# Quantised attention on one Trainium2 core: where a unit's second half of values is multiplied

## The chip, the core and the metric

The kernel runs on one core of a Trainium2 chip. The core has five engines that run side by side, each with its own queue in order: TensorE (PE, matrix products into PSUM; its weight loads are listed apart as PEld), VectorE (DVE), ScalarE (ACT), GpSimd (POOL) and SyncE (SP), which here issues the DMA transfers. They wait for each other by semaphores. The metric is the device time of one execution in microseconds, lower is better.

## What is computed

Two layers of a perceiver: a float cross attention with 16 heads of 128, a channel-mixing layer, an expert layer, then in the second layer a cross attention whose operands are quantised, a dilated self attention and a feed-forward in a block format. The part that the change touches is the quantised cross attention:

```python
q = _fq_sym(q, axis=-1)          # 16 heads of 16
k = _fq_sym(k, axis=-1)
v = _fq_sym(v, axis=2)
attn = jnp.einsum('bhqd,bhkd->bhqk', q, k)
attn = jax.nn.softmax(attn.astype(jnp.float32), axis=-1)
attn = _fq_unsigned(attn, axis=-1)       # 0..255 steps of the row's largest
out = jnp.einsum('bhqk,bhkd->bhqd', attn, v)
```

There are 2 batches of 128 queries, 16 heads, and 4096 keys (the contexts of both batches together).

## The kernel before, in words

A unit is one batch and one head: 32 units, of 128 queries against 4096 keys. Their stage runs from about 456 us to 658 us of the span; before it lies the float cross attention, behind it a tail. Work on a unit has these steps:

- **First scores** (`pe_first`, L1845): TensorE computes the scores in 8 blocks of 512 keys, each into one of three PSUM banks; VectorE reduces each block to the rows' largest value (`dve_first`, L1889, reduction at L1891). These run ahead: in quarter q of unit u TensorE computes blocks 8u+12+2q and the next, that is blocks of units u+1 and u+2. A bank is written again when the reduction three blocks earlier has ended (`q_max`).
- GpSimd folds the eight values into the exponential's bias (L2009 to L2016).
- **Second scores** (`pe_second`, L1861): TensorE computes the same scores again, 1024 keys (a quarter) at a time, into one of two pairs of banks; ScalarE makes the exponential of the quarter (L1884) into a row buffer of halves (`y`, in the space named cT in the profile), two quarters to a half. The quarter two later may be computed when this exponential has ended (`q_exp`).
- **Transposition**: when both quarters of a half are there, SyncE issues a DMA transpose of 128 x 2048 values (L1979) into `yT` (in the space named c_nat). Its landing is told by one of four semaphores, q_turned00 to q_turned11: parity of the unit, then half.
- **Values** (`attend`, product at L1907): 16 matmuls of 128 x 16 for each half, which add up in PSUM bank 7. This is done two units behind: in unit u for unit u-2. All score matmuls are recorded at L1842, first and second alike.

TensorE's order is written out in `pe_attention` (L1895): unit by unit, four quarters each, in each quarter two second-score matmuls, two first-score matmuls, then what else belongs there. Between these steps lies a second program, `side`, whose pieces have slots in quarters 1 to 3 of each unit and work on other layers: mixing, experts and queries of batch 1, then the output, the dilated attention and the feed-forward of batch 0. In quarter 0 TensorE only waits there for the engine that empties the last piece's room in bank 7. ScalarE, VectorE and GpSimd weave their parts of `side` in the same way. SyncE's own queue also loads weights for later in units 0 to 4 (`sp_ahead`, L1449 to L1454).

Units are counted below as the loop does (u from 1); the values multiplied in unit u are those of unit u-2.

Of the kernel before, what the change touches and what calls it, by code (L numbers as in the profile page):

```python
# [43 lines left out]
UNITS = B * H0  # L44
# [20 lines left out]
NH = KT * P // HALF  # L65
# [415 lines left out]
def pe_idle_product(pe, m, ps):  # L481
    return pe.matmul(ps, m.ident_fp16[:, :], m.kT[:, 0, 0:BLK], start=True, stop=True)
# [1362 lines left out]
def pe_first(pe, m, s, n):  # L1845

    if n == 0:
        pe.wait_ge(s["exp"], UNITS)
    if n % NB == 0 and n // NB % H1 < KG:
        pe.wait_ge(s[f"qu_act{n // (NB * H1)}"], QU_ACT[f"qT{n // NB % H1}"])  # L1850
    if n > 2:
        pe.wait_ge(s["q_max"], n - 2)
    pe_scores(pe, m, n // NB, m.bank(n % 3), n % NB * BLK).then_inc(s["q_first"], 1)
# [7 lines left out]
def pe_second(pe, m, s, u, q):  # L1861

    n = NC * u + q
    if u == 0 and q > 0:
        pe.wait_ge(s["q_exp"], q)
    elif n == NC:
        pe.wait_ge(s["q_exp"], NC)
    elif n > NC:
        pe.wait_ge(s["q_exp"], n - 1)
    if n == NC + 1:  # L1870
        pe.wait_ge(s["added"], UNITS)
    for k in range(CHUNK // BLK):
        ins = pe_scores(pe, m, u, m.bank(second_place(u, q) + k), q * CHUNK + k * BLK)
    ins.then_inc(s["q_second"], 1)
# [20 lines left out]
def pe_attention(pe, m, x, s, side):  # L1895
    def attend(z, half):
        b, h = z // H1, z % H1
        if z < UNITS - 1:
            pe.wait_ge(s[f"q_turned{z % 2}{half}"], 16 * (z // 2 + 1))
        else:  # L1900
            pe.wait_ge(s["q_back_dve"], NB // 2 if half == 0 else BACK_DVE)
        if z == UNITS - 1 and half == 1:
            pe.wait_ge(s["q_back_act"], NB - BACK_DVE)
        if z in (H1, H1 + H1 // 2) and half == 0:
            pe.wait_ge(s["at_dve0"], AT_DVE["over_sum1" if z > H1 else "over_sum0"])
        for j in range(KT // NH):
            ins = pe.matmul(m.bank(7)[:, h * HD1:(h + 1) * HD1], x.yT[:, z % 2, half * KT // NH + j, :],  # L1907
                            m.v_int[:, half * KT // NH + j, h * HD1:(h + 1) * HD1], start=half == 0 and j == 0,
                            stop=half == 1 and j == KT // NH - 1)
        ins.then_inc(s["q_pv"], 1)  # L1910

    def turn(n):

        pe.wait_ge(s["q_exp"], NC * (UNITS - 1) + n * BLK // CHUNK + 1)
        if n == 3:
            pe.wait_ge(s["q_back_dve"], 1)
        if n == 0:
            pe.wait_ge(s["q_max"], NB * UNITS)
        y = m.y[:, (UNITS - 1) % 2, n * BLK:(n + 1) * BLK]
        for j in range(BLK // P):  # L1920
            ins = pe.matmul(m.bank(back_bank(n))[:, j * P:(j + 1) * P], y[:, j * P:(j + 1) * P], m.ident_fp16[:, :],
                            start=True, stop=True)
        ins.then_inc(s["q_back"], 1)
        if n == NB - 1:
            pe.wait_ge(s["q_back_dve"], 3)
            for _ in range(2):
                pe_idle_product(pe, m, m.bank(2))

    pe.wait_ge(s["v_rounded_dve"], KT // 4)
    pe.wait_ge(s["v_rounded_pool"], KT // 4)  # L1930
    for u in range(1, UNITS + 2):
        for q in range(NC):
            if u < UNITS:
                pe_second(pe, m, s, u, q)
            for n in range(AHEAD + NB * u + 2 * q, AHEAD + NB * u + 2 * q + 2):
                if n < NB * UNITS:
                    pe_first(pe, m, s, n)
            if q == 0:
                side.upto(NC * u - 0.5)
            if u >= UNITS and q < 2:  # L1940
                for n in range(NB // 4 * (2 * (u - UNITS) + q), NB // 4 * (2 * (u - UNITS) + q + 1)):
                    turn(n)
            if u > 1 and q < 2:
                attend(u - 2, q)
            if q > 0:
                side.upto(NC * u + q)

# [13 lines left out]
def back_bank(n):  # L1961

    return n % 3 if n < NB // 2 else n - 1
# [551 lines left out]
def perceiver(nc, t):  # L2515
    pe, act, dve, pool, sp = nc.tensor, nc.scalar, nc.vector, nc.gpsimd, nc.sync
    with ExitStack() as stack:
# [28 lines left out]
        with ExitStack() as local:  # L2546
# [13 lines left out]
                pool_output(pool, m, y, a, s, 0, 1, room, output), pool_dilated(pool, m, s, 0, room, dilated),  # L2560
                pool_feed(pool, m, w, s, 0, room, feed), pool_output(pool, m, y, a, s, 1, 0, room, output_last)))
            pe_attention(pe, m, y, s, Side(
                pe_mix(pe, m, x, s, 1, room, mix), pe_experts(pe, m, s, 1, room, experts, a.expert_wT),
                pe_queries(pe, m, s, 1, room, queries), pe_output(pe, m, y, a, s, 0, 0, room, output),
# [71 lines left out]
```

## Time and profile before

| | |
|---|---|
| median of 3 runs | 691.06 us (691.05 to 693.09) |
| profiled execution | 691.99 us, of which the traced span is 690.6 us |
| busy in the span | PE 94%, DVE 83%, ACT 60%, POOL 57% |
| chain of waits over the span | PE 64%, DVE 17%, ACT 5%, DMA 5%, POOL 4% |
| attention stage, 560 to 652 us (92 us) | PE busy 83.7, DVE 87.5, ACT 83.3, POOL 42.8 |

Busy time of PE counts overlapping matmuls as one stretch and their ends are modelled, so a busy PE is not necessarily a full one. The chain of waits is followed back from the last instruction: each step is what released it. A row of the chain "PE psum L1842 x4" is four score matmuls in a row.

### The profile page before, as it was taken

How to read it: one execution, taken by the hardware profiler on the slowest of the kernel's cores; microseconds unless marked ns; L12 is line 12 of the kernel's file. 1: busy time of each engine (PE TensorE's matmuls, PEld its weight loads, DVE VectorE, ACT ScalarE, POOL GpSimd, SP SyncE). 2: the span in 40 equal slices, each digit the busy share in tenths (PEclk: the TensorE clock that was granted, in tenths of full speed). 3: DMA queues.
4: the chain of work that ended last, by engine and by line, in shares of the span. 5: the costliest groups of instructions: out<-in, count | busy, mean ns of one | idle time of the engine just before them, and what ended most of it. 6: DMA issues, size and time to landing. Idle time of an engine off the chain costs nothing.

```text
span 690.6 us, 13892 instructions
## 1 busy us (share of the span) xinstructions
PE 651.4 (94%) x5088; PEld 410.2 (59%) x5088; DVE 575.2 (83%) x1029; ACT 417.4 (60%) x695; POOL 391.5 (57%) x504
## 2 busy tenths in 40 slices
PE   9899999999999999989999999989889989988887
PEld 7456666667666676756776667754346434544453
DVE  5998987897798797889989769888877889999655
ACT  5654454444544465655574445448878889899941
POOL 5877666577557627689956515527634543345401
PEclk9999999999999999999999999999999999999999
DMA  9666789756647689988885984739998989999900
GB/s 314 155 149 127 164 176 180 164 137 144 138 117 154 144 177 224 208 186 178 163 182 124 184 173 110 157 81 211 222 207 153 165 139 203 167 182 164 196 19 9
DMA packets 347971, 111.27 MB, mean 161 GB/s; under 512 B 313592, under 2 KB 344576, under 8 KB 347904
## 3 DMA queue, kind: packets, MB, share of 16 engines
q1 hardware_dynamic: 347904, 110.39, 77.6%
q8 instruction: 41, 0.67, 0.4%
q14 instruction: 26, 0.21, 0.1%
HBM read 32.23 MB, written 0.26 MB: 47 GB/s over the span
## 4 chain that ended last, share of the span: by engine, by line
PE 64%; DVE 17%; ACT 5%; DMA 5%; POOL 4%; issue 3%; SPq 2%; POOLq 0%; ACTq 0%; DVEq 0%
PE psum L1059 19%; PE psum L1031 18%; DVE tops L1891 7%; PE psum L1842 6%; PE psum L1045 5%; PE psum L506 3%; ACT cT L1884 3%; PE psum L1907 2%; DMA wqk_h<-in_wkT 2%; DMA c_nat<-cT 2%; DVE neg_max L1271 1%; DMA c_nat<-in_expert_wT 1%; PE psum L1084 1%; PE psum L1094 1%; PE psum L826 1%
## 5 line engine op out<-in xcount | busy, mean ns | idle before, releaser
L1059 PE MATMUL psum<-c_nat,eT 128*128 128x256 f16 x1536 | 188.1, 273 | 0.9 <-ACT u_sb L1233 0.9
L1891 DVE TENSOR_REDUCE tops<-psum 128x1 f32<-128x512 f32 x256 | 159.6, 683 | 20.2 <-PE psum L1842 19.5
L1884 ACT ACTIVATE cT<-psum,bias,q_scale 128x1024 f16<-128x1024 f32 x128 | 153.7, 1205 | 22.0 <-PE psum L1842 20.3
L1031 PE MATMUL psum<-cT,qk 128*128 128x512 f16 x744 | 165.6, 379 | 0.1
L1059 PEld LDWEIGHTS psum<-c_nat,eT 128*128 128x128 f16 x1536 | 147.3, 98 | 24.1 <-issue 1.6
L1842 PE MATMUL psum<-kT,v_space 128*128 128x512 f16 x512 | 139.5, 387 | 9.2 <-DVE tops L1891 7.3
L1031 PEld LDWEIGHTS psum<-cT,qk 128*128 128x128 f16 x744 | 72.6, 98 | 82.3 <-issue 1.2
L1271 DVE TENSOR_REDUCE neg_max<-psum 128x1 f32<-128x2048 f32 x32 | 73.2, 2287 | 21.9 <-PE psum L1031 21.8
L1259 DVE TENSOR_TENSOR e_lo<-e_all,e_hi 128x2048 f16<-128x2048 f32 x32 | 88.8, 2774 | 0.0
L1842 PEld LDWEIGHTS psum<-kT,v_space 128*128 128x128 f16 x512 | 45.2, 98 | 70.8 <-DVE tops L1891 34.2
L1202 ACT ACTIVATE e_all<-psum,neg_max 128x2048 f32<-128x2048 f32 x32 | 63.1, 1971 | 16.0 <-DVE neg_max L1273 16.0
L857 ACT ACTIVATE qT<-psum 128x128 f32<-128x128 f32 x31 | 8.7, 279 | 103.8 <-PE psum L826 94.2
L775 POOL TENSOR_TENSOR k_full<-k_int,k_scale 128x256 f32<-128x256 bf16 x32 | 21.7, 679 | 70.7 <-DVE k_int L1339 47.0
L1207 ACT CAST e_hi<-e_all 128x2048 f16<-128x2048 f32 x32 | 60.8, 1900 | 1.5 <-DMA eT<-e_hi 0.6
L2011 POOL TENSOR_SCALAR least<-least,tops 128x1 f32<-128x1 f32 x64 | 23.3, 364 | 50.3 <-DVE tops L1891 49.3
L1045 PE MATMUL psum<-wkv,cT 128*128 128x512 f16 x192 | 46.7, 379 | 2.5 <-DVE k_tmp L1325 2.5
L776 POOL TENSOR_TENSOR k_parts<-k_int,k_scale 128x256 f16<-128x256 bf16 x32 | 48.8, 1524 | 0.0
L1907 PEld LDWEIGHTS psum<-v_space,c_nat 128*128 128x128 f16 x1024 | 33.8, 96 | 22.8 <-DMA c_nat<-cT 6.6
L745 POOL TENSOR_TENSOR u_parts<-u_sb,u_parts 128x256 f16<-128x256 f32 x30 | 31.4, 1046 | 24.3 <-ACT u_parts L1238 24.3
L1907 PE MATMUL psum<-v_space,c_nat 128*128 128x16 f16 x1024 | 35.3, 170 | 8.7 <-DMA c_nat<-cT 4.4
L748 POOL TENSOR_TENSOR wvo_parts<-wvo_h,wvo_parts 128x512 f16<-128x512 f32 x30 | 36.6, 1219 | 0.1
L758 POOL TENSOR_TENSOR wqk_parts<-wqk_h,wqk_parts 128x512 f16<-128x512 f32 (+1 forms) x27 | 31.0, 1147 | 2.5 <-ACT wqk_parts L869 2.1
(287 smaller groups left out, 946.9 us busy)
## 6 DMA issues: line engine op xcount, KB each, us to landing
wvo_h<-in_L_xattn_Wv SPq DMA_DIRECT2D x30, 128.0 KB, 2.4
wvo_h<-in_L_xattn_Wo SPq DMA_DIRECT2D x30, 128.0 KB, 2.4
wqk_h<-in_L_xattn_Wq SPq DMA_DIRECT2D x28, 128.0 KB, 2.5
wqk_h<-in_wkT SPq DMA_DIRECT2D x28, 128.0 KB, 2.8
mx_land<-in_mx_weights SPq DMA_DIRECT2D x8, 384.0 KB, 3.8
v_space<-in_ctx SPq DMA_DIRECT2D x4, 512.0 KB, 5.5
cT<-in_ctx SPq DMA_DIRECT2D x2, 1024.0 KB, 8.0
c_nat<-in_expert_wT SPq DMA_DIRECT2D x2, 1024.0 KB, 7.8
```

The source lines that it names most:

```text
L776: pool.tensor_tensor(hi, ints, scale, ALU.mult).then_inc(s["k_cut"], 1)
L1031: ins = pe.matmul(s_ps[:, n * 512:(n + 1) * 512], c.qk[:, u % 2, q_part, k, :], m.cT[:, b, c_part, 4 * n:4 * n + 4, k, :], start=(k, q_par ...
L1045: ins = pe.matmul(kv_ps, m.cT[:, kt // KTB, c_part, kt % KTB, k, :], d.wkv[w_part][:, k, :], start=(k, w_part, c_part) == (0, 0, 0), stop= ...
L1059: ins = pe.matmul(u_ps, c.eT[:, v % 2, e_part, j, :], m.c_nat[:, v // H0, c_part, j, :], start=(j, e_part, c_part) == (0, 0, 0), stop=(j, ...
L1202: act.activation(c.e_all[:, :], s_ps, ACT.Exp, bias=c.neg_max[:, u % 2:u % 2 + 1], scale=1.0 / UP, accum_out=c.row_sum[:, u:u + 1]).then_i ...
L1207: act.copy(c.e_hi[:, :], c.e_all[:, :]).then_inc(s["e_hi"], 1)
L1259: dve.tensor_tensor(c.e_lo[:, :], c.e_all[:, :], c.e_hi[:, :], ALU.subtract).then_inc(s["e_lo"], 1)
L1271: dve.tensor_reduce(limit, s_ps, AX.X, ALU.max, negate=True).then_inc(s["max"], 1)
L1842: return pe.matmul(ps, m.qT[:, b, group, r, :], m.kT[:, group, at:at + BLK], start=True, stop=True)
L1884: act.activation(m.y[:, u % 2, q * CHUNK:(q + 1) * CHUNK], m.bank(second_place(u, q), 2), ACT.Exp, bias=m.bias[:, u:u + 1], scale=m.q_scal ...
L1891: dve.tensor_reduce(m.tops[:, n // NB, n % NB:n % NB + 1], m.bank(n % 3), AX.X, ALU.max, negate=True).then_inc(s["q_max"], 1)
L1907: ins = pe.matmul(m.bank(7)[:, h * HD1:(h + 1) * HD1], x.yT[:, z % 2, half * KT // NH + j, :], m.v_int[:, half * KT // NH + j, h * HD1:(h ...
```

## The change

In `pe_attention` the call that multiplies the second half of unit u-2's values is issued in quarter 0 of unit u, right behind the first half, and no longer in quarter 1. For the two last turns (u = 32 and 33, where no new scores are computed) the halves stay in quarters 0 and 1. Nothing else changes: the instructions, buffers, banks and the other engines' programs are the same.

```diff
-            if u > 1 and q < 2:
-                attend(u - 2, q)
+            for half in range(NH) if 1 < u < UNITS and q == 0 else (q,) if u >= UNITS and q < NH else ():
+                attend(u - 2, half)
             if q > 0:
                 side.upto(NC * u + q)
```

NH is 2, UNITS is 32. So it moves 16 matmuls in each of the 30 units 2 to 31, on TensorE alone.

In TensorE's queue, unit 7 (values of unit 5) before; q_turned10 and q_turned11 are the landings of the two halves:

```order
L1842 MATMUL psum<-kT,v_space 128x512 [waits q_exp]
L1842 MATMUL psum<-kT,v_space 128x512
L1842 MATMUL psum<-kT,v_space 128x512 [waits q_max] x2
L1907 MATMUL psum<-v_space,c_nat 128x16 [waits q_turned10,mix_act1]
L1907 MATMUL psum<-v_space,c_nat 128x16 x15
L1842 MATMUL psum<-kT,v_space 128x512 [waits q_exp]
L1842 MATMUL psum<-kT,v_space 128x512
L1842 MATMUL psum<-kT,v_space 128x512 [waits q_max] x2
L1907 MATMUL psum<-v_space,c_nat 128x16 [waits q_turned11]
L1907 MATMUL psum<-v_space,c_nat 128x16 x15
```

and with the change:

```order
L1842 MATMUL psum<-kT,v_space 128x512 [waits q_exp]
L1842 MATMUL psum<-kT,v_space 128x512
L1842 MATMUL psum<-kT,v_space 128x512 [waits q_max] x2
L1907 MATMUL psum<-v_space,c_nat 128x16 [waits q_turned10,mix_act1]
L1907 MATMUL psum<-v_space,c_nat 128x16 x15
L1907 MATMUL psum<-v_space,c_nat 128x16 [waits q_turned11]
L1907 MATMUL psum<-v_space,c_nat 128x16 x15
L1842 MATMUL psum<-kT,v_space 128x512 [waits q_exp]
L1842 MATMUL psum<-kT,v_space 128x512
L1842 MATMUL psum<-kT,v_space 128x512 [waits q_max] x2
```

The wait for q_turned11 and its 16 matmuls moved ahead of two second-score and two first-score matmuls.

In TensorE's queue, unit 16 (values of unit 14), from a piece of the side program (L2080) on, before:

```order
L2080 MATMUL psum<-wp,xnT 128x256 [waits wp1_scaled,at_act0]
L1842 MATMUL psum<-kT,v_space 128x512 [waits q_exp]
L1842 MATMUL psum<-kT,v_space 128x512
L1842 MATMUL psum<-kT,v_space 128x512 [waits q_max] x2
L1907 MATMUL psum<-v_space,c_nat 128x16 [waits q_turned00,at_act0]
L1907 MATMUL psum<-v_space,c_nat 128x16 x15
L1842 MATMUL psum<-kT,v_space 128x512 [waits q_exp]
L1842 MATMUL psum<-kT,v_space 128x512
L1842 MATMUL psum<-kT,v_space 128x512 [waits q_max] x2
L1907 MATMUL psum<-v_space,c_nat 128x16 [waits q_turned01]
L1907 MATMUL psum<-v_space,c_nat 128x16 x15
L1842 MATMUL psum<-kT,v_space 128x512 [waits q_exp]
```

and with the change:

```order
L2080 MATMUL psum<-wp,xnT 128x256 [waits wp1_scaled,at_act0]
L1842 MATMUL psum<-kT,v_space 128x512 [waits q_exp]
L1842 MATMUL psum<-kT,v_space 128x512
L1842 MATMUL psum<-kT,v_space 128x512 [waits q_max] x2
L1907 MATMUL psum<-v_space,c_nat 128x16 [waits q_turned00,at_act0]
L1907 MATMUL psum<-v_space,c_nat 128x16 x15
L1907 MATMUL psum<-v_space,c_nat 128x16 [waits q_turned01]
L1907 MATMUL psum<-v_space,c_nat 128x16 x15
L1842 MATMUL psum<-kT,v_space 128x512 [waits q_exp]
L1842 MATMUL psum<-kT,v_space 128x512
L1842 MATMUL psum<-kT,v_space 128x512 [waits q_max] x2
L1842 MATMUL psum<-kT,v_space 128x512 [waits q_exp]
```

Here the same four score matmuls moved behind 16 more matmuls of L1907; from the quarter after them on, the queue is as it was.

## Rows read from the trace of the kernel before

**Rows 1.** Stretches of the attention stage: start:end, length, busy time by engine

```profile
core 0: us, PE busy (x) PEld busy (x) DVE busy (x) ACT busy (x) POOL busy (x), PEclk, DMA share, GB/s
...
560.00:652.00 92.00, 83.70 (x818) 41.83 (x817) 87.49 (x169) 83.31 (x147) 42.76 (x105) 0.99 1.04 179
```

**Rows 2.** Costliest groups, 470 to 652 us: | busy us, mean ns | idle

```profile
L1891 DVE TENSOR_REDUCE tops<-psum 128x1 f32<-128x512 f32 x232 | 144.3, 683 | 16.6 <-PE psum L1842 16.1
L1884 ACT ACTIVATE cT<-psum,bias,q_scale 128x1024 f16<-128x1024 f32 x118 | 141.7, 1204 | 16.1 <-PE psum L1842 14.4 <-issue 0.5 <-DMA c_nat<-cT 0.3
L1842 PE MATMUL psum<-kT,v_space 128*128 128x512 f16 x464 | 126.1, 388 | 8.2 <-DVE tops L1891 7.3 <-ACT v_space L1811 0.2 <-ACT cT L1884 0.2
...
L1907 PE MATMUL psum<-v_space,c_nat 128*128 128x16 f16 x933 | 32.2, 170 | 7.6 <-DMA c_nat<-cT 4.4 <-ACT v_space L1811 1.6 <-DVE mid L2303 1.1
```

**Rows 3.** Timeline in unit 16: start, us, engine, line, names, count

```profile
564.55 4.55 DVE L1891 TENSOR_REDUCE tops<-psum 128x1 f32<-128x512 f32 x7
...
565.29 0.56 PE L1907 MATMUL psum<-v_space,c_nat 128*128 128x16 f16 x16
...
565.71 1.02 PE L1842 MATMUL psum<-kT,v_space 128*128 128x512 f16 x4
...
566.57 0.55 PE L1907 MATMUL psum<-v_space,c_nat 128*128 128x16 f16 x16
...
566.97 2.37 PE L1842 MATMUL psum<-kT,v_space 128*128 128x512 f16 x9
```

**Rows 4.** Chain of waits, 510 to 652 us, by line

```profile
by line: DVE tops L1891 32.3%; PE psum L1842 22.7%; ACT cT L1884 8.0%; PE psum L1907 7.0%; PE psum L506 4.0%; issue 3.8%; ACT v_space L1811 1.2%; DVE mx_amax L2233 1.1%; POOL xn L464 0.9%; PE psum L2180 0.9%; DVE mid L2303 0.8%; DVE stats L
```

**Rows 5.** Chain of waits in order: start, us, what

```profile
525.46 0.88 PE psum L1842 x4
526.34 0.38 PE psum L1907 x16
...
565.85 0.68 PE psum L1842 x3
...
566.55 5.54 DVE tops L1891 x9
...
572.82 5.98 DVE tops L1891 x10
```

**Rows 6.** Chain of waits, units 14, 21 and 24

```profile
553.50 0.25 PE psum L1792 x4
...
595.54 0.68 PE psum L1842 x3
...
596.25 0.69 DVE tops L1891
...
613.11 0.46 PE psum L1842 x2
...
613.59 0.97 ACT cT L1884
```

**Rows 7.** Timeline of TensorE, unit 19: a block that waits for its bank

```profile
582.63 0.39 PE L1842 MATMUL psum<-kT,v_space 128*128 128x512 f16 x1 [0.21 <-DVE tops L1891]
```

**Rows 8.** Who waited for whom, 470 to 652 us: total, times, longest

```profile
PE psum L1907 <- DMA c_nat<-cT: 4.4, 4, 2.4
```

**Rows 9.** SyncE's timeline, 483 to 508 us

```profile
497.78 11.32 SPq L1979 DMA_TRANSPOSE c_nat<-cT  x4
```

**Rows 10.** Unit 7: timeline of TensorE

```profile
503.61 1.02 PE L1842 MATMUL psum<-kT,v_space 128*128 128x512 f16 x4
...
507.00 0.56 PE L1907 MATMUL psum<-v_space,c_nat 128*128 128x16 f16 x16 [2.37 <-DMA c_nat<-cT]
```

**Rows 11.** Transpositions (L1979), 510 to 652 us, us to landing

```profile
DMA to landing us min/median/max: 4.2/4.5/6.6
```

**Rows 12.** The one transposition issued at 575.6 us

```profile
DMA to landing us min/median/max: 6.6/6.6/6.6
```

**Rows 13.** Windows: the stretch behind that wait, columns as in rows 1

```profile
507.40:511.70 4.30, 4.30 (x20) 1.63 (x17) 3.00 (x7) 2.87 (x5) 1.79 (x3) 0.60 1.15 232
```

## The prediction

> **What bounds the kernel now.** I read first the busy time by stretch. From 560 to 652 us, 92 us and some 15 units, VectorE is busy 87.5 us, TensorE 83.7 and ScalarE 83.3 [rows 1]: three engines within 5% of each other, none with room for a delay of its own. The groups give the pieces [rows 2]: a reduction of a block takes 683 ns, an exponential 1,204 ns, a score matmul 388 ns and a value matmul 170 ns, but matmuls overlap, so their price must be read from starts.
>
> The timeline of unit 16 does that [rows 3]. The 16 value matmuls of a half start at 565.29 and the next score matmul at 565.71; at 566.57 and 566.97 again. So a half holds TensorE for **0.41 us**. Four score matmuls (a quarter's second and first scores) hold it from 565.71 to 566.57, **0.86 us**. VectorE's row there is 7 reductions in 4.55 us, 0.65 each, near 0.63 where more stand in a row: 1.25 us for the two blocks of a quarter. Thus quarters 0 and 1 take TensorE 0.86 + 0.41 = 1.27 us each, quarters 2 and 3 take 0.86 plus side work. That is just VectorE's 1.25 and ScalarE's 1.2 us. The layout before spreads the halves evenly.
>
> The chain of waits from 510 to 652 us has 32.3% on the reductions, 22.7% on score matmuls, 8.0% on exponentials and 7.0% on value matmuls [rows 4]: it changes engines all the time, and what a delay costs depends on where the chain is between the two halves.
>
> **What the change does.** No instruction is added or removed. In each of 30 units, 16 matmuls, 0.41 us, move ahead of four score matmuls. They are TensorE's only; no DMA is issued otherwise, and SyncE, VectorE, ScalarE and GpSimd keep their order. In quarter 0 TensorE then works 1.68 us and in quarter 1 0.86; behind the old place it is where it was. So quarter 1's second scores (the input of ScalarE's exponential) and first scores (two reductions) come 0.41 us later, and nothing comes earlier except bank 7's sums, for which nobody waits in these units. That has four kinds of outcome.
>
> *The chain stays on TensorE across both places: no cost.* An example is unit 10, with value matmuls, four score matmuls, value matmuls in a row on the chain [rows 5]; the 0.41 us is only reordered. Units 3, 10 to 12, 15, 20 and 27 look like this. I charge 0 for them, and 0 also where VectorE has side work queued (units 13 and 22, whose reductions start over 0.6 us after their scores are there). The cover is the wait of VectorE in quarter 2 that the trace shows in units 10 and 11; without it each would pay up to 0.41.
>
> *The chain leaves TensorE right after the first half, to an engine that waits for it: full price.* In unit 16 the chain goes value matmuls, three score matmuls (565.85), then VectorE at 566.55 for nine reductions in a row, then after a short piece of side work ten more from 572.82 [rows 5]. The third score matmul is the first block of quarter 1. It comes 0.41 us later, and VectorE has nothing else. Unit 21 (595.54 to 596.25) is the same, and in unit 24 two score matmuls release the exponential of quarter 1 at 613.59, from which side work hangs [rows 6]. I find six such units: 16, 21, 24, 25, 26 and 30. 6 x 0.41 = 2.5 us.
>
> *The chain is on VectorE, with TensorE held back by the banks.* A score block may be written when the reduction three blocks back has ended; at that moment VectorE has two blocks ready and gets this one, 3 x 0.63 = 1.9 us of work. Until quarter 1's first block is there TensorE needs 0.21 (this matmul) + 0.41 (first half) + 0.43 (second scores) + 0.38 (the block itself) = 1.43 us, and about 0.2 goes for the signal, as in the row of a block that waits for its bank, 0.21 [rows 7]. That leaves 0.2 to 0.3 us of slack, and 0.41 is asked: 0.2 us lost in each of units 9, 17, 23 and 29, 0.8 us. Where TensorE was a little late already (units 8, 18 and 28) 0.2 to 0.3 each, 0.7 us together. It isn't won back in quarter 2, since there VectorE never waits in these units.
>
> *The second half has not landed.* Four waits of TensorE for a transposition stand in the stage, 4.4 us, the longest 2.4 [rows 8]. They are in units 5 to 7, where SyncE's queue is behind: it issues four transpositions in a row in 11.3 us from 497.78 on [rows 9], long after their exponentials. So these landings don't move with TensorE. In unit 7 TensorE computes quarter 1's four score matmuls at 503.61, then waits for the half until 507.00 [rows 10]. With the change it waits first and has these four left at 507.4: **0.86 us later** for all that follows, since the chain runs over this landing and then on TensorE. In units 5 and 6 the same happens, but SyncE's backlog of over 3 us hides it: 0.
>
> Elsewhere the margin is this. The half's transposition is issued when its last exponential ends and lands 4.5 us later in the median, 6.6 at most [rows 11]. At the new place TensorE stands three quarters of a unit of 6 us plus 1.3 us after that exponential, 5.8 us. Only landings above this are late; the one issued at 575.6 (6.6 us, [rows 12]) is, by some 1.1 us, in unit 19, and a wait of 0.3 us may come in unit 17. In unit 19 VectorE has side work; I charge 0.2 us. On the other side, in unit 14 the chain enters TensorE between the two halves and reaches a product of the side program (553.50, [rows 6]) behind the second: that comes up to 0.41 us earlier; I take 0.2. These two cancel.
>
> **Sum.** 2.5 + 0.8 + 0.7 + 0.9 = +4.9 us. Against the profiled execution, 691.99 us with a span of 690.6, that is 696.9 with a span of 695.5. The profiled one lies 0.9 above the median of 691.06, so for the median I say **696.0 us**. Bounds: only the zero-slack units and unit 7, less 0.8 us for TensorE's shorter way to side work in units 14 and 19, give +2.6; 0.41 in each of 20 units without cover gives 8.2, so 699.3.
>
> A rule speaks against this. The stretch from 560 to 652 us shows weight loads busy 41.8 of 92 us [rows 1]. The Trainium skill (Perfetto Trace Analysis, Identifying the Most-Contended Engine) has TensorE's headroom judged by weight-load busy share and not by matmul busy time. By it TensorE is at 45% and could take 0.41 us anywhere: the sum would be the first rival's. By the rows of starts TensorE is full in quarters 0 and 1, and I go by these.
>
> **Rivals.**
> (1) *The delay is absorbed, no change.* The exponential and the reduction double- and triple-buffer, and VectorE idles 4.5 of the 92 us; if the slack ahead of each reduction is really above 0.41 us, only unit 7 pays: 691.06 + 0.9 = 692.0. Against it: the chain hands over from TensorE to VectorE in units 16 and 21 with no slack. 11%.
> (2) *More transpositions are late, and the clock falls.* Behind the 2.4 us wait of unit 7 TensorE runs 4.3 us at a mean granted clock of 0.60, most of it at the lower level, 1.2 GHz [rows 13]. Three more units wait (15, 17 and 19 have the least margin, 3 x 0.9), and a longer wait in unit 6 brings one more such period, 1.7 us: 4.9 + 2.7 + 1.7, 700.4 us. For it: the wait of unit 6 grows from 1 to about 2 us. Against: SyncE's backlog hides unit 6, and later landings are regular. 10%. The Trainium skill (TensorE: Matmul & The Clock Gate, HAM oscillation) says that waiting for DMA between bursts makes the clock fall each time, at half of the slow period's length; the trace agrees for unit 7, and by it alone unit 6 would add those 1.7 us.
> (3) *Faster.* In the 4.3 us behind unit 7's wait the mean clock of 0.60 costs 4.3 x 0.40 = 1.7 us [rows 13]. TensorE now falls idle 0.86 us earlier; if the period comes that much earlier and lies mostly inside the wait, 1.7 us return, and units 14 and 19 give 0.8. It decides only if the reductions' delays are absorbed as well: 691.06 + 0.9 - 2.5 = 689.5. 4%.
>
> The forecast itself has 75%. Changes under 0.3%, 2.1 us, can't be told from none. Slower by more: nearly all of the forecast (73 of 75) and rival 2: 0.83. Within: rival 1 and the rest: 0.13. Faster: 0.04. Range 691.9 to 699.6: it reaches down to rival 1 and up to the bound of 20 units.
>
> **What would show it.** In the new profile the second half should start 0.41 us after the first in nearly all units, and L1842's first matmuls of quarter 1 0.41 us later against the first half. VectorE's and ScalarE's idle time for "PE psum L1842" should grow by 4 to 8 us together with the span, that of the value matmuls for the transposition from 4.4 to 6 or 7 us. The span from 510 to 652 us should carry four fifths of the loss and unit 7 the rest. If VectorE's waits do not grow, the bank argument is wrong; if the value matmuls' DMA waits grow by far more than 3 us, rival 2; if the reductions start as early against the first half as before, rival 1.

## The result, and the profile after

The changed kernel takes 695.57 us (median of 5 runs, 695.40 to 697.81) against 691.05 us before (5 runs, 688.04 to 693.09): ratio 1.0087, 95% interval 1.0068 to 1.0106. It is slower, 4.5 us by the medians; 4.9 us and 696.0 us were forecast. The profiled execution took 695.40 us, its span is 694.1 us.

The spans alone (690.6 and 694.1) would give 3.5 us. But the attention stage did not start at the same time: the first value matmul, which the change leaves where it is, starts at 471.93 us before and at 470.19 us after, 1.74 us earlier, through the stages ahead, which the change doesn't touch. In the ten profiles of the experiments below the start of the stage moves by -1.8 to +0.9 us (in e5_both1, where this matmul is moved too, read from the first exponentials). So two profiles are compared here from that matmul on: how much later does the first value matmul of each unit start? By this measure the stage lost **5.24 us** up to unit 32, and from there to the end the two traces agree to 0.01 us. All times of value matmuls below are those of the matmul itself; its weight load can start up to 0.2 us ahead of it.

The stretches of the changed kernel (start:end length, then busy time of PE, PEld, DVE, ACT, POOL, then clock, DMA share, GB/s):

```profile
560.00:652.00 92.00, 82.59 (x788) 40.50 (x784) 86.04 (x164) 80.82 (x144) 40.81 (x101) 0.98 1.00 173
```

Against [rows 1] all engines are less busy in the same 92 us: TensorE 82.6 for 83.7, VectorE 86.0 for 87.5, ScalarE 80.8 for 83.3. Nobody works more; all wait more. Who waits is in the costliest groups of the stage:

```profile
L1891 DVE TENSOR_REDUCE tops<-psum 128x1 f32<-128x512 f32 x228 | 142.7, 683 | 22.3 <-PE psum L1842 20.9
L1884 ACT ACTIVATE cT<-psum,bias,q_scale 128x1024 f16<-128x1024 f32 x114 | 136.7, 1202 | 23.4 <-PE psum L1842 22.2
L1842 PE MATMUL psum<-kT,v_space 128*128 128x512 f16 x455 | 123.7, 389 | 7.9 <-DVE tops L1891 6.3 <-ACT midT L2494 0.3 <-ACT v_space L1811 0.3
...
L1907 PE MATMUL psum<-v_space,c_nat 128*128 128x16 f16 x928 | 28.0, 169 | 8.6 <-DMA c_nat<-cT 5.7 <-ACT v_space L1811 1.6 <-DVE mid L2303 1.1
```

VectorE's idle time ahead of its reductions for a score matmul grew from 16.1 to 20.9 us, ScalarE's ahead of its exponentials from 14.4 to 22.2 us, the value matmuls' for a transposition from 4.4 to 5.7 us [rows 2].

Unit 16, the example of [rows 3, 5], in the timeline of the changed kernel:

```profile
564.79 2.05 DVE L1891 TENSOR_REDUCE tops<-psum 128x1 f32<-128x512 f32 x3
...
565.56 0.95 PE L1907 MATMUL psum<-v_space,c_nat 128*128 128x16 f16 x32
...
566.36 3.18 PE L1842 MATMUL psum<-kT,v_space 128*128 128x512 f16 x12
...
566.99 1.20 ACT L1884 ACTIVATE cT<-psum,bias,q_scale 128x1024 f16<-128x1024 f32 x1 [0.32 <-PE psum L1842]
567.21 2.48 DVE L1891 TENSOR_REDUCE tops<-psum 128x1 f32<-128x512 f32 x4 [0.38 <-PE psum L1842]
```

The 32 value matmuls now stand in a row, 565.56 to 566.36, 0.80 us where a half took 0.41. The reductions, seven in a row before, break off after three: VectorE idles 0.38 us, ScalarE 0.32 us, both until the score matmuls that come behind.

Unit 7 on TensorE:

```profile
502.45 0.55 PE L1907 MATMUL psum<-v_space,c_nat 128*128 128x16 f16 x16
505.62 0.56 PE L1907 MATMUL psum<-v_space,c_nat 128*128 128x16 f16 x16 [2.62 <-DMA c_nat<-cT]
506.04 5.39 PE L1842 MATMUL psum<-kT,v_space 128*128 128x512 f16 x15
511.63 0.39 PE L1842 MATMUL psum<-kT,v_space 128*128 128x512 f16 x1 [0.21 <-DVE tops L1891]
511.86 0.95 PE L1907 MATMUL psum<-v_space,c_nat 128*128 128x16 f16 x32
```

No score matmuls lie any more between the two halves; the wait for the landing is 2.62 us for 2.37 [rows 10], and 16 score matmuls are left behind it until unit 8 instead of 12. The clock falls as before:

```profile
506.00:511.40 5.40, 5.27 (x23) 1.79 (x19) 3.49 (x7) 3.91 (x7) 2.39 (x6) 0.68 1.04 210
```

In this stretch the mean granted clock is 0.68; behind the same wait it was 0.60 over 4.3 us [rows 13]. Both stretches begin behind the wait and hold the whole slow time: it cost 4.3 x 0.40 = 1.7 us before and 5.4 x 0.32 = 1.7 us after, so nothing came back from it. SyncE's queue is as it was, behind in units 2 to 7:

```profile
494.15 1.03 SPq L1452 DMA_DIRECT2D wp<-in_L_xattn_Wp  x1
495.23 0.47 SPq L1453 DMA_DIRECT2D bp<-in_L_xattn_bp  x1
495.74 0.43 SPq L1454 DMA_DIRECT2D sets<-in_dil_sets  x1
496.27 20.50 SPq L1979 DMA_TRANSPOSE c_nat<-cT  x7
```

These are three weight loads, 2.1 us of queue, and behind them seven transpositions in a row. From 510 to 652 us the transpositions land as in [rows 11], and the one that took 6.6 us in [rows 12] took 4.6 here:

```profile
DMA to landing us min/median/max: 4.6/4.6/4.6
```

### The profile page after: what moved, and what is told of

Read it like the earlier page. It is cut to its first block and busy times, and to the rows that moved or that the text cites. A ratio compares the mean times of both kernels' runs of the same rounds, so it can differ in the third digit from the quotient of the medians.

```text
span 694.1 us, 13892 instructions
## 1 busy us (share of the span) xinstructions
PE 651.5 (94%) x5088; PEld 409.4 (59%) x5088; DVE 575.7 (83%) x1029; ACT 417.6 (60%) x695; POOL 390.8 (56%) x504
## 5 line engine op out<-in xcount | busy, mean ns | idle before, releaser
L1202 ACT ACTIVATE e_all<-psum,neg_max 128x2048 f32<-128x2048 f32 x32 | 63.0, 1970 | 16.2 <-DVE neg_max L1273 16.1
L1907 PE MATMUL psum<-v_space,c_nat 128*128 128x16 f16 x1024 | 31.2, 169 | 9.8 <-DMA c_nat<-cT 5.7
L1907 PEld LDWEIGHTS psum<-v_space,c_nat 128*128 128x128 f16 x1024 | 29.9, 96 | 16.9 <-DMA c_nat<-cT 6.2
L1233 ACT ACTIVATE u_sb<-psum,inv_sum 128x256 f32<-128x256 f32 x32 | 15.2, 474 | 27.9 <-PE psum L1059 27.9
```

The lines of the kernel that those rows point to most:

```text
L1202: act.activation(c.e_all[:, :], s_ps, ACT.Exp, bias=c.neg_max[:, u % 2:u % 2 + 1], scale=1.0 / UP, accum_out=c.row_sum[:, u:u + 1]).then_i ...
```

## The experiments

My theory: the price is the 0.41 us of value matmuls that go ahead of quarter 1's scores, less the slack that is there, unit by unit; only in units 4 to 7 is it the landing. The first rival: TensorE pays for waiting two by two for landings, everywhere. The second: any burst of matmuls costs by its length or by the switch of kind. All kernels are edits of `pe_attention` alone, where nothing else is said. The times are medians. The ratio, with its 95% interval, is to runs of the kernel before beside it on the same chip; it is not the ratio of the two medians and differs from it by up to 0.2%. The median of the kernel before was 690.40 us beside the first four kernels, 690.78 beside the next four and 689.99 beside the last two.

**e1_wait.** TensorE waits as in the change, but its matmuls stay.

```diff
             if u > 1 and q < 2:
                 attend(u - 2, q)
+            if 1 < u < UNITS and q == 0:
+                pe.wait_ge(s[f"q_turned{u % 2}1"], 16 * ((u - 2) // 2 + 1))
```

> The old order, and TensorE only waits for the second half's landing in quarter 0 already, behind the first half's matmuls; the 16 matmuls stay in quarter 1. So it has the change's waits without its matmuls. Theory (the moved 0.41 us of matmuls is the price nearly everywhere, a landing only in units 4 to 7): 1 to 2 us slower than before, 692 to 693, and the loss is complete by unit 8; behind unit 8 no unit adds over 0.1 us. Rival (TensorE waits for transpositions, at all units): about the full loss of the change, 694.5 to 696, growing from unit to unit.

Measured: 692.21 us, ratio 1.0027 (1.0006 to 1.0049). In the profile unit 8 starts 1.96 us late, and behind it no unit adds more than 0.01 us until unit 15. There it gains 1.13 us, which is no merit of the edit: before, TensorE runs at the lower clock from 559.2 us on,

```profile
559.20:562.60 3.40, 3.40 (x28) 1.46 (x25) 1.86 (x5) 2.37 (x5) 1.10 (x3) 0.50 0.65 123
```

and in this execution it didn't. In return it fell in the early units, where the two waits stand:

```profile
489.28 0.56 PE L1907 MATMUL psum<-v_space,c_nat 128*128 128x16 f16 x16 [1.51 <-DMA c_nat<-cT]
490.81 1.89 PE L1842 MATMUL psum<-kT,v_space 128*128 128x512 f16 x4 [0.98 <-DMA c_nat<-cT]
```

```profile
488.00:497.00 9.00, 6.75 (x47) 3.00 (x48) 4.54 (x8) 6.10 (x12) 4.56 (x12) 0.62 1.02 227
```

The score matmuls of 490.81 took 1.89 us for four, where four take 1.02 us at full clock; over the 9 us the mean clock is 0.62. Behind unit 15 one more unit pays, unit 17, 0.41 us: its half landed 5.6 us after its issue, and TensorE waited.

```profile
569.96 1.04 PE L1842 MATMUL psum<-kT,v_space 128*128 128x512 f16 x4 [0.42 <-DMA c_nat<-cT]
```

So waiting alone costs 2 us in units 4 to 7, and here 0.4 us in unit 17, which my expectation (no unit over 0.1 us) had not allowed; the other units pay nothing. The rival "landings everywhere" is out. How much of the 2 us is waiting is less sure: the landing that unit 7 waits for comes 0.98 us later against the first value matmul than before, and in e9_mixed, which keeps the old order there, it comes 0.33 us later too. Between that landing and unit 8 another 0.98 us are added, and these belong to the wait's new place.

**e2_early** and **e3_late** split the change at unit 8.

```diff
+            for half in range(NH):
+                if u > 1 and q == (0 if u < 8 else half):             # e2_early
+                if u > 1 and q == (0 if 7 < u < UNITS else half):     # e3_late
+                    attend(u - 2, half)
```

> The new order in units 2 to 7 alone, the old one from unit 8 on. Theory: the landings that come late through SyncE's backlog lie here, 1 to 2 us slower than before, 692 to 693, all of it at unit 8, nothing behind. Rival (matmuls alone count, evenly, 0.17 us a unit): 6 x 0.17 = 1.0 us spread evenly over units 2 to 7. Rival (a waiting TensorE brings slow clock periods that cost most): the new order brings one more period at the lower clock here and 3 us or more.

> The old order in units 2 to 7, the new one in units 8 to 31. Theory: 4.9 less 1 to 2 us, so 3 to 4 us slower than before, 694 to 695; about 0.4 us in each of units 16, 21, 24, 25, 26 and 30, 0.2 in 9, 17, 23 and 29, none in 10 to 13, 20 and 22, a gain in 14, 15 and 19. Rival (the late landings make the loss): within 1 us of before.

Measured: e2_early 692.90 us, ratio 1.0028 (1.0010 to 1.0047); unit 8 starts 2.31 us late, the rest adds -0.12. e3_late 694.39 us, ratio 1.0056 (1.0034 to 1.0078); unit 8 at -0.03, the end at +3.49. The parts, 2.2 and 3.5 us, make 5.7 against 5.2 for the whole. Units 8 to 31 of e3_late came out as they do in the changed kernel, most to 0.01 us. e2_early's 2.31 us are a little over the 1 to 2 us expected, without one more period at the lower clock.

**e4_eight** moves half of the matmuls.

```diff
+            elif u > 1 and q == 0:
+                attend(u - 2, 0)
+                attend(u - 2, 1, 0)      # matmuls 0 to 7 of the second half
+            elif u > 1 and q == 1:
+                attend(u - 2, 1, 1)      # matmuls 8 to 15
```

> Only 8 of the second half's 16 matmuls go to quarter 0, the other 8 stay in quarter 1, in all units. The wait for the landing is in quarter 0 as in the changed kernel. Theory (price = inserted time less the slack at hand): half the price, 0.2 us, in the six units without slack (16, 21, 24, 25, 26, 30), 0 to 0.05 in the units with about 0.17 us of slack (9, 17, 23, 29), and the late landings of units 4 to 7 as with all 16: 1.2 + 0.2 + 0.3 + 1.5, about 3 us slower than before, 694. Rival (the price is linear, no slack): the late units cost half of their 3.3 to 4 us. Rival (each switch between kinds of matmul costs): with one switch more than the changed kernel it is as slow as that or slower, 695.5 or more.

Measured: 693.81 us, ratio 1.0043 (1.0021 to 1.0065). The units, in us, with the charge of unit u read as what it adds to the start of unit u+1's first value matmul:

| units | forecast | changed | e3_late | e4_eight | e8_loads_new |
|---|---|---|---|---|---|
| 2 to 7 | 0.9 | 1.91 | -0.03 | 1.69 | -1.76 |
| 16, 21, 24, 25, 26, 30 | 2.5 | 2.31 | 2.32 | 1.12 | 2.30 |
| 9, 17, 23, 29 | 0.8 | 0.93 | 0.98 | 0.38 | 0.92 |
| 8, 18, 28 | 0.7 | 0.82 | 0.84 | 0.32 | 0.82 |
| 14, 15, 19 | 0.0 | -0.81 | -0.71 | 1.40 | -0.80 |
| 27 | 0.0 | 0.21 | 0.21 | 0.01 | 0.22 |
| the other seven | 0.0 | -0.12 | -0.12 | 0.00 | -0.12 |
| sum | 4.9 | 5.24 | 3.49 | 4.93 | 1.58 |

With half the matmuls the six units without slack pay 0.19 or 0.20 each (0.13 in unit 16, which pays 0.32 in the changed kernel), half of 0.40; units 9, 23 and 29 pay 0.03 where they paid 0.23 (17, with a landing near its limit, pays 0.29). Both fit one slack of 0.17 us that is used up first: 0.40 - 0.17 = 0.23 and 0.20 - 0.17 = 0.03. The linear price is out, and so is the price per switch, since this kernel has one switch more. By the medians the kernel is 3.4 us slower than before and by the ratio 3.0 us, as I had summed up. The profiled execution, 695.80 us, is 2.0 us above its own median; its 4.93 us hold one unit that isn't of this kind:

```profile
582.14 0.55 PE L1908 MATMUL psum<-v_space,c_nat 128*128 128x16 f16 x16
583.27 0.36 PE L1908 MATMUL psum<-v_space,c_nat 128*128 128x16 f16 x8 [0.58 <-DMA c_nat<-cT]
583.49 1.87 PE L1842 MATMUL psum<-kT,v_space 128*128 128x512 f16 x4
```

In unit 19 the half landed late (this transposition took 6.5 us), TensorE waited 0.58 us, and the four score matmuls behind took 1.87 us: the clock had fallen, to a mean of 0.53 from 583.4 to 587.0 us. Unit 19 cost 1.60 us, where the changed kernel had gained 0.44.

**e5_both1** moves the first half back instead.

```diff
+            for half in range(NH):
+                if u > 1 and q == (1 if u < UNITS else half):
+                    attend(u - 2, half)
```

> The mirror image: both halves in quarter 1, none in quarter 0, in units 2 to 31. Theory (a half of 0.41 us is paid where the chain leaves TensorE right behind it): the six units that paid in full for the change (16, 21, 24, 25, 26, 30) now gain up to 0.4 us each, since the first half too goes out of the way of quarter 1's scores; units whose chain goes to a piece of the side program behind quarter 1 (10, 11, 12, 14, 19, 20) pay up to 0.4, so do units where VectorE or ScalarE waits for quarter 2. Together near 0, 689 to 692, with both signs by unit. Rival (two halves back to back are bad anywhere, by the length of the burst): about as slow as the changed kernel, 694 to 696, no unit faster.

Measured: 694.88 us, ratio 1.0039 (1.0021 to 1.0057): slower, and outside what I had said. Here the start of each unit's last exponential is the measure, as the value matmuls themselves are moved. The six units changed by +0.04, 0.00, -0.04, +0.08, 0.00 and -0.14 us: only unit 30 gained a little. Over the whole stage this measure gives +2.65 us, as the ratio does (2.7). The gain I expected is not there: no slack toward later is not the same as a gain toward earlier.

**e7_loads** and **e8_loads_new** take the landings' lateness away: SyncE issues the three weight loads behind unit 8, not 4 (in `sp_ahead`), with the old and with the new order.

```diff
-    elif n == AHEAD_PARTS:
+    elif n == 8:
```

> The old order of matmuls; SyncE's three loads behind unit 4 (wp, bp, sets, 2.2 us of its queue) are issued behind unit 8. Theory (landings are late in units 5 to 7 through SyncE's backlog): the second half of unit 5's values lands up to 2.2 us earlier, unit 7 no longer waits 2.4 us, 1.5 to 3 us faster than before, 687.5 to 689.5, and no period at the lower clock at unit 8. Rival (the transposition itself is slow there, DMA bandwidth): the landing comes at the same time, no change.

> The changed kernel's order with the three loads issued behind unit 8. Theory: the part of the loss that came from landings (units 4 to 7, 1.9 us with the change) shrinks to under 1 us, the part of the moved matmuls in units 8 to 31 (3.3 to 3.5 us) stays: 3.5 to 4.5 us slower than the same loads with the old order. Rival (the loss needs the late landings everywhere): the difference to the same loads with the old order falls under 1 us.

Measured: e7_loads 688.72 us, ratio 0.9971 (0.9955 to 0.9988); e8_loads_new 692.04 us, ratio 1.0030 (1.0014 to 1.0045). In unit 7 of e7_loads no wait is left, and SyncE's ten transpositions follow each other:

```profile
503.26 0.55 PE L1907 MATMUL psum<-v_space,c_nat 128*128 128x16 f16 x16
503.66 1.02 PE L1842 MATMUL psum<-kT,v_space 128*128 128x512 f16 x4
504.52 0.55 PE L1907 MATMUL psum<-v_space,c_nat 128*128 128x16 f16 x16
```

```profile
490.09 26.18 SPq L1979 DMA_TRANSPOSE c_nat<-cT  x10
516.32 0.69 SPq L1452 DMA_DIRECT2D wp<-in_L_xattn_Wp  x1
```

Unit 7 alone is 3.27 us shorter: the 2.4 us of waiting and a part of the 1.7 us that the clock behind it cost. It is 3.27 us shorter in the profiles of e10_best and e11_loads_again too. Between the two kernels lie 4.3 us by the profiles from the first value matmul on (+1.58 and -2.72), 4.1 us by the ratios and 3.3 us by the medians; 3.5 to 4.5 were expected. Of the 4.3 us, 0.4 lie in units 2 to 7, as expected under 1 us. The new order's charges in units 8 to 31 are 3.34 us with late landings or without (changed kernel and last column of the table): they don't need them. The other 0.6 us are no charge of the order: in e7_loads the slow stretch of units 14 and 15 lies elsewhere (last section), which made these two 0.54 us shorter.

**e9_mixed** chooses by unit.

```diff
+            for half in range(NH):
+                if u > 1 and q == (0 if u in (10, 11, 14, 19) else 1 if u in (16, 21, 24, 25, 26, 30) else half):
+                    attend(u - 2, half)
```

> A placement by unit: both halves in quarter 0 in units 10, 11, 14 and 19, which gained 0.09, 0.09, 0.30 and 0.44 us from it; both in quarter 1 in units 16, 21, 24, 25, 26 and 30, where the chain leaves TensorE behind the first half; one in each elsewhere. Theory: 0.9 + up to 2.4 us faster than before, 687.2 to 689.6. Rival (the layout before is a balance and any burst costs): 690.5 or more, the six units slower than before.

Measured: 689.98 us, ratio 0.9982 (0.9969 to 0.9995), just outside the theory's range. Units 10, 11 and 14 gained 0.09, 0.09 and 0.30 us as they did in the change; the six units gained nothing here either (by the last exponentials 0.00 in 21 and 26, 0.08 to 0.36 late in the others), and unit 19 lost 1.4 us:

```profile
578.91 0.56 PE L1907 MATMUL psum<-v_space,c_nat 128*128 128x16 f16 x16 [0.50 <-DMA c_nat<-cT]
579.33 1.75 PE L1842 MATMUL psum<-kT,v_space 128*128 128x512 f16 x4
```

It is the picture of e4_eight: a landing after 6.5 us, a wait of 0.50 us, and four matmuls at the lower clock. But this execution has no slow stretch in units 14 and 15 (mean clock 1.00 from 553 to 563 us), and unit 15 is 1.26 us shorter by its last exponential than before: in this profile the two nearly cancel, so unit 19 doesn't explain by itself why the kernel stayed short of the theory.

**e10_best** puts together what had held: the loads behind unit 8 and both halves in quarter 0 in units 10, 11 and 14. **e11_loads_again** is e7_loads a second time.

```diff
+                if u > 1 and q == (0 if u in (10, 11, 14) else half):
```

> SyncE's three loads behind unit 8, and both halves in quarter 0 in units 10, 11 and 14 only, the others as before. Theory (prices add up by unit): the loads' gain and 0.09 + 0.09 + 0.30 us more, 0.5 us less than the loads alone, 688 to 689, faster than before and than the changed kernel. Rival (the gains of single units are given back at the next unit): the same as the loads alone.

> The old order with the three loads behind unit 8, a second time, as the measure for the kernel beside it. Theory: again 2 to 2.7 us faster than before; in the profile no wait over 2.3 us for a transposition in unit 7. Rival (the first profile was lucky with its landings): within 1 us of before.

Measured beside each other: e10_best 686.87 us (684.88 to 689.78, 12 runs), ratio 0.9953 (0.9936 to 0.9969); e11_loads_again 687.41 us (686.23 to 689.23, 12 runs), ratio 0.9959 (0.9945 to 0.9973). Both beat the kernel before (689.99 us there), and by these ratios against 1.0087 the changed kernel. e10_best lies below the 688 to 689 us expected; 0.5 us less than the loads alone came out by the medians. Units 10, 11 and 14 bring 0.47 us in e10_best's profile, and units 12 and 13 behind them give nothing back, but the intervals of the two kernels overlap: the loads are shown as a gain, the three units only by the traces.

## Why the prediction was right, and where it was off

- *Quarter 1's scores come 0.41 us later and nothing comes earlier*: right. The 32 matmuls stand in a row, and the delay is passed to ScalarE and VectorE in unit 16 as 0.32 and 0.38 us.
- *Full price in six units, 2.5 us*: right, 2.31 us: 0.40 in five of them and 0.32 in unit 16. e4_eight shows that the size of the inserted block sets it.
- *0.2 us in each of four units through the banks' slack, 0.8 us*: right in kind, 0.93 us measured, 0.23 each; the slack is 0.17, not 0.2 to 0.3.
- *0.7 us in units 8, 18 and 28*: 0.82 (0.39, 0.32 and 0.11).
- *No cost in units 3, 10 to 12, 15, 20 and 27, whose chain stays on TensorE*: right for all but unit 27, which paid 0.21 us, and 0.01 with half of the block. It belongs to the units with a slack of 0.2 us.
- *The half that has not landed, 0.9 us*: this term was mis-sized, 1.91 us in units 2 to 7. Of it 0.36 us is that the landing itself comes later (505.62 for 507.00 - 1.74 = 505.26); e9_mixed, with the old order there, has 0.33 us of this as well, so it is within what executions differ by. Unit 7 had started 0.99 us late; the backlog hid the rest of that, as forecast. From there to unit 8's value matmuls it takes 6.24 us instead of 4.69 (505.62 to 511.86; before from 507.00 to the row below), 1.55 us more. The four score matmuls are 0.86 of this. The rest is VectorE: while TensorE waits it now has no blocks of quarter 1, and before 511.03 and 511.63 TensorE waits for its reductions in turn. I had counted TensorE's lost time alone.

```profile
511.69 0.55 PE L1907 MATMUL psum<-v_space,c_nat 128*128 128x16 f16 x16
```

- *Units 14 and 19 cancel to zero*: off by 0.8 us with unit 15. Unit 14 gained 0.30 and unit 15 0.08 us (the latter is not stable, +0.03 in e3_late). Unit 19 gained 0.44 in the three profiles with the new order in which its second half was there in time: a product of the side program (L2167) stands behind the second half's old place, and TensorE comes to it 1.98 us behind the unit's first value matmul and not 2.38. In the changed kernel the transposition of [rows 12] took 4.6 us. In e4_eight and e9_mixed it took 6.5 us and unit 19 cost 1.4 to 1.6 us. The late landing of this unit was put at "some 1.1 us" beyond the margin; 6.6 less 5.8 is 0.8.
- The two errors, +1.0 and -0.8, nearly cancel in the sum: 4.9 forecast, 5.24 measured in the stage, 4.5 between the medians. That the forecast met the median so well is partly luck.
- *The signs*: VectorE's and ScalarE's idle time for score matmuls grew by 4.8 and 7.8 us (4 to 8 forecast); that of the value matmuls for the transposition went to 5.7 us, just under the 6 or 7. Of the loss 64% lie in units 8 to 31 and 36% ahead of them, not four fifths and one.
- Rival 1 (absorbed) is out: the waits grew as foretold. By weight-load busy share TensorE had room, 40.5 of 92 us, and still five units paid in full. The Trainium skill (Perfetto Trace Analysis, Identifying the Most-Contended Engine) judges TensorE's headroom by this share, beside the share of its peak FLOPs that a kernel reaches. It does not say that a block may therefore go anywhere; that was my step, and the measurement decides against it, since the share is a mean over the stretch and not the order in one quarter.
- Rival 2's mechanism is real, at another place: not unit 6 but unit 19, in some executions. The changed kernel's profile shows no additional slow period, so it is not the cause of the loss: unit 6 waits 1.20 us for its second half, not 2, and the clock stays up.

```profile
488.00:505.00 17.00, 11.85 (x120) 6.30 (x120) 11.45 (x19) 12.88 (x24) 6.99 (x18) 1.00 1.13 215
```

In unit 19 a slow period follows a wait of 0.58 us (e4_eight) or 0.50 us (e9_mixed). The Trainium skill (TensorE: Matmul & The Clock Gate, HAM oscillation) describes a kernel in which the clock falls at every wait for DMA between bursts; its waits are longer than these. Here it fell behind the 2.37 us of unit 7 and the two of unit 19, and not behind the 1.20 us, so "each time" does not hold in this kernel.
- Rival 3 (faster) is out: the slow period lies behind the wait's end, all of it, and not inside it.

What stays open: why e5_both1 is 2.7 us slower by its ratio (4.1 us by the medians), spread over many units (0.59 us in unit 29, 0.39 in 14, 0.36 in 8); only that the six units gain nothing is shown. And why units 14 and 15 differ among executions beyond the clock of the slow period there.

## What to carry to other kernels

When three engines are within 5% of each other, the order within a fraction of a microsecond is the schedule: a block of 0.41 us that moves ahead of work that another engine waits for costs 0.41 us less the slack there, though no instruction is added. Moving a block away from such work need not give the same back: in e5_both1 and e9_mixed it gave nothing. Take the price from starts and from the chain of waits at each place, and compare two profiles from a common instruction on: here the stages ahead had shifted by 1.74 us, a third of what the change is worth. And look for the queue that makes a transfer late before moving the work that waits for it: postponing three loads of 2.1 us gave back 3.3 us in one unit and 0.3 to 0.4% of the kernel's time.

## What the hardware showed that I had not expected

- A unit's charge repeats from execution to execution to 0.01 us where no transfer and no clock change is in it (units 20 to 31 of e3_late and the changed kernel), while whole runs of one kernel spread over 5 us.
- The clock fell behind a wait of TensorE of only 0.50 us (e9_mixed) or 0.58 us (e4_eight), but not at the 1.56 us wait of unit 15 (for ScalarE, not for a DMA) in e1_wait's execution, where it did in the kernel before. In e7_loads it fell ahead of that place, at 550.1 us, and no wait within 5 us before it was longer than 0.62 us:

```profile
547.43 0.39 PE L1842 MATMUL psum<-kT,v_space 128*128 128x512 f16 x1 [0.62 <-DVE tops L1891]
...
550.00:553.60 3.60, 3.60 (x24) 1.50 (x21) 2.53 (x5) 2.50 (x5) 0.96 (x3) 0.53 0.97 185
```

- An unchanged program has its slow stretches at other places in other executions, so a unit in which one lies can't be compared between two profiles by its length alone.
